# A four-layer graph network on one NeuronCore: VectorE's dependent pairs split into steps, two layers normalised and added in one pass, layer 3's inverses spread by DMA, new instruction orders

## What is computed

```python
# layer 0: 8 heads of 32, q = k = v = LN(h)*g1+be1; masked softmax; residual; LN; MLP 256-1024-256 with gelu
scores = einsum('bhqd,bhkd->bhqk', qkv, qkv) / sqrt(32); attn = softmax(where(adj > 0, scores, -inf))
x = x + attn @ qkv;  x = x + gelu(LN(x) @ W1 + b1) @ W2 + b2
# layers 1 and 2: graph attention, 4 heads of 64
e = leaky_relu(s_src[:, :, None, :] + s_dst[:, None, :, :], 0.2);  att = softmax(where(adj > 0, e, -9e15))
h_prime = einsum('bijh,bjhd->bihd', att, x @ W)
# layer 3: 4 heads of 64 with q, k, v, o projections, mask adj | eye
out = relu((softmax(where(mask, q @ k.T / 8, min)) @ v) @ Wo + bo)
```

## Time and profile before

| | us |
|---|---|
| median of 3 runs | 4592.98 (4592.07 to 4594.39) |
| the profiled execution | 4593.01 |
| its span, first to last instruction | 4591.2 |
| TensorE busy | 4197.4 (91%) |
| VectorE busy | 3338.9 (73%) |
| ScalarE busy | 2186.3 (48%) |
| GpSimd busy | 474.9 (10%) |
| mean granted TensorE clock | 0.964 |
| mean DMA rate | 39 GB/s |

### The profile page before, as it was taken

How to read it: one execution, slowest core, us unless ns; L and a number is a source line. 1 busy time by engine, 2 the same in 40 slices (tenths; PEclk the granted TensorE clock), 3 DMA queues, 4 the chain that set the end, 5 groups by cost and what they waited for, 6 DMA issues and landing times.

```text
span 4591.2 us, 59287 instructions
## 1 busy us (share of the span) xinstructions
PE 4197.4 (91%) x23076; PEld 1974.8 (43%) x23108; DVE 3338.9 (73%) x6505; ACT 2186.3 (48%) x3361; POOL 474.9 (10%) x469
## 2 busy tenths in 40 slices
PE   6789999999999999999999999999999999999997
PEld 2344444344444444444444443444443444444443
DVE  5587767887677877677877677877678776778755
ACT  3444445544445544455544455444455444555433
POOL 0011110111100111101111101111001111011100
PEclk9899999999999999999999999999999999999998
DMA  2011110111110111100111101111101111011100
GB/s 78 19 42 47 47 44 12 38 47 46 47 38 19 38 47 47 47 28 19 47 47 47 46 17 31 47 47 47 41 16 38 47 47 47 28 28 38 47 24 19
DMA packets 202072, 176.87 MB, mean 39 GB/s; under 512 B 142912, under 2 KB 176960, under 8 KB 193344
## 3 DMA queue, kind: packets, MB, share of 16 engines
q1 hardware_dynamic: 201792, 173.07, 12.6%
HBM read 122.17 MB, written 17.30 MB: 30 GB/s over the span
## 4 chain that ended last, share of the span: by engine, by line
PE 59%; DVE 26%; ACT 6%; POOL 4%; issue 3%; DMA 1%; SPq 0%; POOLq 0%; ACTq 0%; DVEq 0%
DVE PG L973 10%; PE M L392 10%; PE M L405 10%; PE M L458 5%; PE S L325 5%; PE O L338 5%; DVE st L808 4%; PE O L444 4%; PE M L416 4%; PE S L491 3%; PE O L507 3%; PE M L469 2%; ACT PP L594 2%; PE O L349 2%; POOL rs L1083 2%
## 5 line engine op out<-in xcount | busy, mean ns | idle before, releaser
L444 PE MATMUL O<-PG,V 128*32 128x512 f32 x4096 | 586.2, 653 | 122.9 <-DVE PG L973 106.1
L973 DVE SCALAR_TENSOR_TENSOR PG<-g,tcg,mT 128x512 f32<-128x512 f32 x1024 | 694.7, 745 | 1.8 <-PE O L448 1.6
L594 ACT ACTIVATE PP<-S,reach 128x1024 f32<-128x1024 f32 x512 | 542.4, 1110 | 239.9 <-PE S L325 181.3
L860 DVE TENSOR_TENSOR PP<-PP,mT 128x1024 f32<-128x1024 f32 x512 | 600.0, 1219 | 40.3 <-ACT PP L594 35.6
L1081 POOL TENSOR_SCALAR ve<-mv 128x4 f32<-128x4 f32 x192 | 160.5, 836 | 3507.1 <-DVE mv L810 3484.7
L392 PE MATMUL M<-hT,W 128*128 128x512 f32 x1024 | 469.0, 607 | 4.9 <-ACT hT L628 1.7
L405 PE MATMUL M<-W,H 128*128 128x256 f32 x2048 | 464.6, 378 | 0.0
L929 DVE TENSOR_TENSOR x<-x,M 128x256 f32<-128x256 f32 x128 | 52.1, 407 | 564.7 <-PE M L405 564.7
L618 ACT ACTIVATE z<-x,nb,rs 128x256 f32<-128x256 f32 x384 | 215.6, 595 | 421.2 <-DVE nb L844 421.2
L405 PEld LDWEIGHTS M<-W,H 128*128 128x128 f32 x2048 | 378.2, 190 | 61.0 <-issue 10.6
L325 PE MATMUL S<-hT 32*128 32x512 f32 x2048 | 297.8, 651 | 30.2 <-ACT PP L594 25.4
(11 more groups left out here) (136 smaller groups left out, 5651.1 us busy)
## 6 DMA issues: line engine op xcount, KB each, us to landing
g<-t_rows SPq DMA_DIRECT2D x64, 1024.0 KB, 4.7
g<-adj_in SPq DMA_DIRECT2D x32, 1024.0 KB, 6.5
x<-x_in SPq DMA_DIRECT2D x32, 512.0 KB, 5.0
out<-x SPq DMA_DIRECT2D x32, 512.0 KB, 3.4
W<-w_in SPq DMA_DIRECT2D x1, 3072.0 KB, 16.0
mT<-V SPq DMA_TRANSPOSE x128, 2.5
m<-hT SPq DMA_TRANSPOSE x128, 2.5
PG<-w_in SPq DMA_DIRECT2D x1, 1280.0 KB, 9.2
```

The source lines that it names most:

```text
L444: e.matmul(k.O[0][r:r + 32, :], s.V[:, jt, 64 * hh + 32 * v:64 * hh + 32 * v + 32], p[:, u, :], start=(jt == 0), stop=(jt == NT - 1))
L594: e.activation(p[:, 2 * pair:2 * pair + 2, :], k.S[:, 2 * pair:2 * pair + 2, :], ACT.Exp, bias=k.reach[:, 7:8], scale=SC0).then_inc(k.e0.s ...
L860: e.tensor_tensor(p[:, 2 * pair:2 * pair + 2, :], p[:, 2 * pair:2 * pair + 2, :], s.mT[:, jt:jt + 1, :].to_broadcast([128, 2, N]), ALU.mul ...
L973: e.scalar_tensor_tensor(out=p[:, u, :], in0=s.T[hh], scalar=s.tcg[:, 1, hh, jt:jt + 1], in1=s.mT[:, jt, :], op0=ALU.max, op1=ALU.mult).th ...
```

## The change

Seven places are changed.

1. `stats` is gone. `bst(b,i,t)` takes the statistics and `bag(b,i,t)` the aggregate, as two steps of VectorE's order, so that other steps can stand between; `bag` waits for its own `bst` through a recorded count (`mark`, `marked`). `i` numbers the six norms.
2. The reciprocal of `b2r` is a step `rc` of its own.
3. In the layers 1 and 2 `b2r` no longer writes `V`: four instructions, one for each head of 64 columns, multiply by the inverse and add to `x`. `fin` remains for layer 0 alone.
4. Layer 3: the 16 columns of inverses are transposed once to 16 rows (`rd3`), copied by ScalarE to `s.tr`, written to DRAM (`rrow`) and read back by two broadcasts, each to 64 partitions (`rbc`). One product of 128x1024 (`rb3`) takes the place of two.
5. The orders on TensorE, ScalarE and VectorE are new. Layer 0's `b2r(.,0,2)`, `(.,0,3)`, `pj(.,2,2)`, `(.,2,3)`, `pv3(.,0)`, `sc3(.,2)` and VectorE's work on them have moved over the end of the loop body; `gvals(b2,2)`, `gw(b2,2,0)` and `gw(b2,2,1)` stand among the adds of `w2`; `gprep(b2,2)` stands ahead of the gelus on ScalarE; `grow(b2,2)` stands ahead of `w2(b1,0)` on TensorE.
6. GpSimd's steps come in the same order as before; only the loop's start is moved.
7. SP: `rrow(b3)`, `trow(b2,2)`, `rbc(b3)`, `tbc(b2,2)`, `store(b3)`, `load(b0)`, `trow(b1,1)`, `tbc(b1,1)`, `masks_t(b0,..)`.

```diff
-            s.rd = sb(f"rd{k}", [128, NT, 4])
+            s.rd = sb(f"rd{k}", [128, 4, NT])
...
 class Pe
+    def rd3(self, b):
+        self.wait_ge(*k.r3.at(b, 0))
+        self.take("M1", k.rdc.at(b, 0))
+        e.transpose(k.M[1][0:16, 0:128], s.rd[:, :, :].rearrange("p h t -> p (h t)"),
+                    k.ident[:, :]).then_inc(k.rd3.sem, 1)
...
 class Act
+    def rd3(self, b):
+        self.wait_ge(*k.rd3.at(b, 0))
+        e.copy(s.tr, k.M[1][0:16, 0:128]).then_inc(k.rdc.sem, 1)
...
 class Dve
+    def bst(self, b, i, t):
...
+        self.mark(e.bn_stats(s.st[:, t, :], src[:, t, :]), "sums", i, b, t)
+    def bag(self, b, i, t):
+        self.marked("sums", i, b, t)
         r = e.bn_aggr(s.mv[:, t, :], s.st[:, t, :])
...
+    def rc(self, b, L, t):
+        self.wait_ge(*k.b2r[L].at(b, t))
+        if L:
+            self.mark(e.reciprocal(s.ri[:, t, 0:4], M[:, 256:260]), "inverse", L, b, t)
...
+    def b2r(self, b, L, t):
+        self.marked("inverse", L, b, t)
+        if L:
+            for h in range(4):
+                x = s.x[:, t, 64 * h:64 * h + 64]
+                r = e.scalar_tensor_tensor(out=x, in0=M[:, 64 * h:64 * h + 64], scalar=s.ri[:, t, h:h + 1], in1=x,
+                                           op0=ALU.mult, op1=ALU.add)
+            r.then_inc(k.add[L].sem, 1)
...
+    def rb3(self, b):
+        self.wait_ge(*k.oc3.at(b, 1))
+        self.wait_ge(*k.lt3.at(b))
+        e.tensor_tensor(s.hT[:, :, :], s.g[:, 0:2, :], s.rb, ALU.mult).then_inc(k.o3.sem, 1)
...
 class Sp
+    def rrow(self, b):
+        self.wait_ge(*k.rdc.at(b, 0))
...
+        e.dma_start(k.t_d[b % NS, 0].rearrange("h (t i) -> (h t) i", t=NT), s.tr).then_inc(k.lw3.of(b), 16)
+    def rbc(self, b):
+        self.wait_ge(*k.lw3.at(b))
+        for h in range(2):
+            rows = k.t_d[b % NS, 0].rearrange("(c h) i -> h c i", h=2)[h]
+            e.dma_start(s.rb[64 * h:64 * h + 64, :, :], rows[None, :, :].to_broadcast([64, 2, N])).then_inc(k.lt3.of(b), 16)
```

More of the change, by code:

```diff
@@ L189, in __init__ @@
          self.gelu, self.pjc, self.gtc, self.spc, self.goc, self.god, self.qka, self.vva, self.e3, self.oc3,
-         self.od3, self.rbc, self.qt, self.sc0, self.pv0, self.dn0, self.b2r, self.tt, self.w1, self.w2, self.pj,
-         self.srt, self.gpv, self.qk, self.vp, self.sqm, self.sc3, self.pv3, self.dn3, self.den3, self.rb3,
+         self.od3, self.rdc, self.qt, self.sc0, self.pv0, self.dn0, self.b2r, self.tt, self.w1, self.w2, self.pj,
+         self.srt, self.gpv, self.qk, self.vp, self.sqm, self.sc3, self.pv3, self.dn3, self.den3, self.rd3,
          self.wo, self.rs, self.parg) = [signal(name) for name in SIGNALS]
@@ L283, in den3, with rd3, rrow, rbc @@
     def den3(self, b): pass
-    def spread3(self, b): pass
-    def rb3(self, b, pr): pass
+    def rd3(self, b): pass
+    def rrow(self, b): pass
+    def rbc(self, b): pass
+    def rb3(self, b): pass
     def wo(self, b, tp): pass
@@ L1162, in tensor_program @@
         b0, b1, b2, b3 = it, it - 1, it - 2, it - 3
+        do.pv3(b3, 0)
+        do.b2r(b1, 0, 2)
+        do.sc3(b3, 2)
+        do.b2r(b1, 0, 3)
+        do.pv3(b3, 1)
+        do.pj(b2, 2, 2)
+        do.pj(b2, 2, 3)
         do.sc3(b3, 3)
-        do.pv3(b3, 1)
+        do.dn3(b3, 0)
+        do.pv3(b3, 2)
         do.prep_b(b1)
@@ L1175, in tensor_program @@
         do.w1(b1, 5)
+        do.den3(b3)
+        do.rd3(b3)
         do.w1(b1, 6)
-        do.pv3(b3, 3)
         do.w1(b1, 7)
+        do.grow(b2, 2)
         do.w2(b1, 0)
-        do.dn3(b3, 1)
-        do.grow(b2, 2)
         do.w2(b1, 1)
-        do.den3(b3)
         do.w2(b1, 2)
-        do.rb3(b3, 0)
-        do.rb3(b3, 1)
         do.w2(b1, 3)
@@ L1253, in tensor_program @@
         do.b2r(b0, 0, 1)
-        do.pv3(b2, 0)
-        do.b2r(b0, 0, 2)
-        do.b2r(b0, 0, 3)
-        do.sc3(b2, 2)
-        do.pj(b1, 2, 3)
 def scalar_program(do):
@@ L1264, in scalar_program @@
         b0, b1, b2, b3 = it, it - 1, it - 2, it - 3
-        do.out3(b3, 0)
+        do.pj(b2, 2, 3)
         do.sc3(b3, 3)
+        do.ln2(b1, 0)
+        do.ln2(b1, 1)
+        do.ln2(b1, 2)
+        do.ln2(b1, 3)
+        do.tt(b1, 0, 0)
+        do.gprep(b2, 2)
+        do.tt(b1, 0, 1)
         do.w1(b1, 0)
+        do.out3(b3, 1)
         do.w1(b1, 1)
@@ L1272, in scalar_program @@
         do.w1(b1, 5)
+        do.rd3(b3)
         do.w1(b1, 6)
+        do.grow(b2, 2)
         do.w1(b1, 7)
-        do.gprep(b2, 2)
-        do.out3(b3, 1)
-        do.grow(b2, 2)
-        do.spread3(b3)
         do.lnz(b1, 1, 0)
```

358 lines of the change are left out of this document (192 added, 166 removed).

## The result

The changed kernel takes 4719.9 us (median, 4713.4 to 4729.2) against 4593.4 of the kernel before: a ratio of 1.028, interval 1.026 to 1.030. It is slower by 126 us where 78 us less were forecast. The slower case of the prediction, x landing late, is not the reason either. The profiled execution took 4715.8, its span 4714.0.

A forecast was written before the change was run, and what follows sets the result against it. TensorE's own work was taken to set the period, apart from a mid-iteration bubble and small waits; 2.7 us an iteration over some 31 iterations, 83.7, less 6 at the end, took 4593.0 to 4515, range 4430 to 4590.

The forecast's parts named there:

- x landing late: Rival: VectorE meets x late at gprep(b1,1); at 9.0 us after issue, 1.3 us an iteration lost, 4639; chance 0.10 slower.
- LN2: At the seam: tt(b1,0) waits about 1.0 us, pv3(b3,3) hides open copies; 0.1 us an iteration gained.
- POOL: GpSimd's steps: nb(b0,0) again waits some 1.2 us beside masks; order of steps kept, effect 0.
- The clock: Around the bubble before gpv(b1,1,0): clock falls as before, once an iteration, and gpv(b1,1,0) takes its 5.38 us.
- Inverses: Layer 3's transposes on TensorE: 1.2 us gained each iteration; 6 us lost in all at the program's end.
- Cost 0: Layer 3's inverses by DMA (rrow, two rbc, rb3): covered by other work in the loop, 0 us.
- Spacing: VectorE's path to gw(b1,1,0): about seven separated dependent pairs save 0.11 us each, 0.7 us an iteration.
- Spacing gives nothing: Rival: no VectorE operation starts before the one ahead ends; 1.3 us an iteration left, 4559; chance 0.12.
- Four pieces of 64: Layers 1 and 2's normalise-and-add on VectorE: four pieces take 0.55 us where 0.34 stood, 0.4 added before gw(b1,1,0).
- The bubble: TensorE's idle stretch before gpv(b1,1,0): this starts 28.0 us after the last W2 matmul instead of 29.3, gain 1.3.
- The range: Whole kernel's time: 4430 (clock stays up, a further us an iteration) to 4590 (without the slower case).

The follow-up runs named there:

- e1: GpSimd's gmax reduction replaced by a copy of the same 4 columns: changed kernel 4482.9 us (0.977), kernel before 4587.7 us (0.999).
- e6: Changed kernel with gprep(b2,2) moved behind what pv3 needs, and layer 3's inverses made the old way, without rrow and rbc: 4509.0 us, ratio 0.982.
- e2: Changed kernel with gprep(b2,2) moved behind layer 3's mask product and pa3 on VectorE, and behind tt(b1,0,1) on ScalarE: 4481.7 us, ratio 0.976.
- e3: As e2, with SP issuing rbc(b3) ahead of trow(b2,2): 4469.3 us, ratio 0.973.
- e7: As e2, with spacing undone: each aggregate right behind its statistics, each reciprocal right ahead of its b2r: 4591.5 us, ratio 1.000.
- e10: Kernel before with three of each four aggregates one VectorE step behind their statistics, nothing else: 4541.7 us, ratio 0.990.
- e8: As e2, with layers 1 and 2 normalised by one instruction for a tile and added by another, as before: 4486.5 us, ratio 0.976.
- e9a: As e3, with layer 1's exponents ahead of b0's statistics, nb(b0,0) ahead of the masks, gout(b2,2,1) behind ln0 on ScalarE: 4563.2 us, ratio 0.994.

## Why the prediction was wrong

*The step that failed* is in the part on LN2: "`pv3(b3,3)` then hides the copies that stood open", with POOL's "Its steps keep their order: 0". The walk followed TensorE up to the first of `tt(b1,0)` and was right so far: forecast 14.2 after the seam, measured 2339.54 - 2325.37 = 14.17, with 0.16 of wait where about 1.0 was forecast. It then gave `pv3(b3,3)` no price. Its own numbers had one: statistics 2.9 us later put the end of `rs(b1,2)` from 10.1 to 13.0 after the seam (measured 12.8), GpSimd's 5.81 and the reduction's 0.39 make 19.2 (measured 19.1), `gprep` and the first product 1.8 more; TensorE is through with `tt` at 15.9. So 5 us, which the trace gave as 4.92. The wait of GpSimd for nothing that shows, 183.8 us in 31 times, was in the waits of before. It was passed over since nobody on the path felt it, and the moved step was costed on its own engine alone.

*The clock.* The forecast kept one fall in an iteration. The new hole brought a second: 7.69 us at 0.61. Of the 237 us between the changed kernel and e1, the waits at L512 are 151. TensorE is busy for 81 us more with the same program of matmuls (4199.2 against 4118.2, mean clock 0.944 against 0.966), so the rest is the low clock, most of it behind that hole: `pv3` alone has 50.7 of the 81.

*Inverses*: right. 1.2 by 31 less 6 is 31.2, and e6 gives 27.3 against e2 and 39.7 against e3. Forecast "Cost 0" for their way by DMA was off by 12 us in 31 iterations (e3 against e2): the 1 MB of layer 2, issued right behind the two of 256 KB, lands in 7.0 us where it was 4.7. The forecast took 4.7 for it, as if it were alone.

*Spacing*: the mechanism was right and the size far off, by the number of pairs that count: 0.7 us an iteration was forecast, 3.5 measured (e7 against e2), 1.4 of it clock, and 1.6 for the aggregates in the order of before (e10, 49 us over 31). The rival "Spacing gives nothing" is out.

*Four pieces of 64*: forecast 0.55 for a tile, from the slope of two rows; the instruction takes 0.27 each, 1.09 busy for a tile with its overlaps counted twice. That is well above the value taken, and the one pass gives nothing (e8).

*The bubble*: `gpv(b1,1,0)` was forecast at T+28.0. It came at 2412.57, T+30.0, in the changed kernel, where the 1.47 at `wo` stand in between, and at 2419.15 in e3, which has no wait there and whose last W2 matmul ends at 2391.12: T+28.0, as forecast. There `gw(b2,2,3)` started at T+15.0, 0.4 ahead of the forecast, and `gw(b1,1,0)` at T+27.2 as forecast, though the pieces of 64 took some 0.6 more than the sum gave them; these errors cancel, so the exact hit is in part luck. The clock fell as forecast.

*x late*: x was waited for 16 times, 1.4 us at the longest, 11.3 us in all. Not the cause.

*The range.* Its lower end is worked out wrongly: another us an iteration below 4469 is 4438, not 4430. Nothing hangs on it.

*Adding up.* The mended kernel with all else as in the change, e2, is at 4482, where the forecast, without the trap, had 4515. Spacing brought 110 us where the sum had 22, which is 88 more, so the rest of the change (`grow`, orders, inverses, one pass) gave some 55 us less than forecast: e7, which has everything but the spacing, is no faster than the kernel before. In it TensorE is busy for 33 us less than before (4164.0 against 4197.4) and idle for 32 us more. Which of the moved steps brought these waits was not separated.

## What to carry to other kernels

When a step of the bound engine is moved up, work out not only when its operand was ready before, but every instruction ahead of it in its producer's queue, and what the first of those waits for. A long wait "for nothing that the profile shows" on an idle engine is a price that waits for a taker. In a queue of short dependent operations on VectorE, first put an independent one between each pair: it changed no work and gave 1% by itself in the kernel before. Parts of a change that pull against each other hide each other's size, so each is run alone.

## What was not expected of the hardware

- GpSimd needs 5.7 to 6.6 us, about 5.9 in the median, from an ordinary operation to the start of a reduction over the partitions whose input is there, 31 times in each kernel that has the reduction. It needs 6.6 to 7.8 us from the reduction back to an ordinary operation (31 times in e9a, median 7.2). With a copy in its place there is neither, and where the input comes 10 us late the change costs nothing more. What it does in that time the rows do not show.
- The Trainium skill, GPSIMD Engine Reference, "Instruction dispatch", gives about 6 us, with no instruction in the profile, for the first call of newly loaded code. The 5.7 to 6.6 agree in size, but here they are paid at the reduction 31 times, and something like them on the way back, not once. Whether it is the same thing no run here shows.
- A pair of dependent operations on VectorE costs about 0.11 us more than a separated one. Separating 33 pairs of an iteration took 110 us off, 66 of TensorE's idle and 44 of its busy time, although VectorE is busy for only 72% of the span.
- A broadcast of 1 MB issued right behind two of 256 KB landed in 7.0 us; issued 4.4 us after them, when they had landed, or without them, in 4.7.
- TensorE's clock after 4.9 us of idleness in a stretch that had been at 1.00: the next 7.69 us at 0.61, mostly the lower of its two levels (1.2 GHz).
- `STT` with 64 columns takes 0.27 us, more than half of the 0.41 that 256 columns take in `TENSOR_TENSOR`.
